# Layer-0 attention: maximum units two to a stretch of scores, one unit's weighing moved, maxima turned in the output bank, inverses in halves

## The reference, cut to what matters

```
q, k, v = x @ w_q, x @ w_k, x @ w_v          # 16 heads of 64
dot = (q / 8) (k / 8)^T                    # scale 1/sqrt(64) on both
att = softmax(where(causal, dot, -inf))
out = att @ v;  return out @ w_u + b_u
x = x + layernorm(attention(layernorm(x)))
```

## Time and profile before

| | before |
|---|---|
| time of three runs, median (lowest to highest) | 2432.9 us (2432.2 to 2436.88) |
| the profiled execution: time, span of its trace | 2433.75 us, 2432.0 us |
| PE busy, share of the span | 2176.9 us, 90% |
| DVE, ACT, POOL busy | 1454.1, 1212.4, 1039.8 us (60%, 50%, 43%) |
| PE busy in 60 to 1080 us, where the pairs run | 954.78 of 1020 us |
| POOL, DVE, ACT busy there | 700.24, 709.24, 514.57 us |

### The profile page before, as it was taken

How to read it: one execution, slowest core, us unless ns; L and a number is a source line. 1 busy time by engine, 2 the same in 40 slices (tenths; PEclk the granted TensorE clock), 3 DMA queues, 4 the chain that set the end, 5 groups by cost and what they waited for, 6 DMA issues and landing times. The chain is left out here.

```text
span 2432.0 us, 41391 instructions
## 1 busy us (share of the span) xinstructions
PE 2176.9 (90%) x15940; PEld 1427.7 (59%) x15940; DVE 1454.1 (60%) x3248; ACT 1212.4 (50%) x1788; POOL 1039.8 (43%) x980
## 2 busy tenths in 40 slices
PE   4999999999999999996899999969999998897787
PEld 2555565555655565554788888734444455555667
DVE  3577757777677757772556665655565455656533
ACT  2455544555365544541333333257787876664533
POOL 0577766777576766774232232423332321100001
PEclk9999999999999999998899999979999999999999
DMA  2000000000000000000300000000000000002001
GB/s 75 1 1 1 1 1 1 1 1 1 2 1 1 1 1 1 1 1 1 73 1 1 1 1 1 1 1 1 1 1 1 1 1 1 2 8 70 1 1 35
DMA packets 36327, 18.26 MB, mean 8 GB/s; under 512 B 16666, under 2 KB 33956, under 8 KB 36132
## 3 DMA queue, kind: packets, MB, share of 16 engines
q1 hardware_dynamic: 36132, 15.61, 2.5%
HBM read 13.50 MB, written 2.10 MB: 6 GB/s over the span
## 5 line engine op out<-in xcount | busy, mean ns | idle before, releaser
L331 POOL TENSOR_TENSOR a_first<-a_first,a_ring 128x512 f32<-128x512 f32 (+3 forms) x352 | 556.4, 1581 | 289.2 <-PE a_o_ps L511 248.4
L1820 ACT ACTIVATE g_probsT<-g_s_ps 128x1024 f32<-128x1024 f32 (+2 forms) x448 | 369.0, 869 | 136.9 <-PE g_s_ps L1689 82.6
L608 ACT ACTIVATE a_ring<-a_st 128x768 f32<-128x768 f32 (+1 forms) x256 | 228.2, 918 | 118.4 <-PE a_st L496 117.1
L511 PE MATMUL a_o_ps<-a_ring,a_v 128*64 128x512 f32 (+3 forms) x1280 | 231.7, 483 | 2.9 <-POOL a_ring L313 2.8
L699 DVE RECIPROCAL a_row_inv<-a_row_inv 128x512 f32<-128x512 f32 x64 | 214.1, 3345 | 20.9 <-ACT a_row_inv L596 20.9
L1090 ACT ACTIVATE m_silu<-m_up,m_b 128x512 f32<-128x512 f32 x160 | 109.8, 689 | 220.4 <-PE m_up L1022 217.6
L1720 PE MATMUL g_o_ps<-g_probsT,g_values 128*32 128x512 f32 (+5 forms) x2688 | 206.7, 419 | 5.5 <-POOL g_probsT L1565 5.1
L684 DVE CUSTOM_DVE_ANT_0 a_masked<-a_mx,mask_wide,a_part_max 128x256 bf16<-128x256 f32 (+3 forms) x256 | 128.4, 548 | 128.3 <-PE a_mx L467 128.3
L467 PE MATMUL a_mx<-a_k_hi,a_q_hi 64*128 64x512 f32 (+3 forms) x768 | 155.1, 419 | 51.6 <-DVE a_largest L684 24.0
L1689 PE MATMUL g_s_ps<-g_qT,g_kT 64*128 64x512 f32 (+3 forms) x896 | 173.5, 434 | 27.5 <-ACT g_probsT L1820 21.4
L1565 POOL TENSOR_SCALAR_AFFINE_SELECT g_probsT<-g_probsT 128x512 f32<-128x512 f32 x128 | 88.2, 692 | 244.9 <-ACT g_probsT L1820 244.8
(11 more groups left out here) (315 smaller groups left out, 4470.4 us busy)
## 6 DMA issues: line engine op xcount, KB each, us to landing
m_w<-in_L_ffn_rw SPq DMA_DIRECT2D x2, 1024.0 KB, 8.3
s_w<-in_L_ffn_w SPq DMA_DIRECT2D x1, 2048.0 KB, 9.6
s_w<-in_L_ffn_w SPq DMA_DIRECT2D x4, 512.0 KB, 10.4
out_x<-x SPq DMA_DIRECT2D x8, 256.0 KB, 2.3
m_w<-in_L_ffn_rw SPq DMA_DIRECT2D x2, 512.0 KB, 5.2
x<-in_L_attn_x SPq DMA_DIRECT2D x1, 512.0 KB, 4.6
a_outT<-in_L_attn_w_q SPq DMA_DIRECT2D x1, 512.0 KB, 5.3
a_outT<-in_L_attn_w_k SPq DMA_DIRECT2D x1, 512.0 KB, 6.0
```

The source lines that it names most:

```text
L331: pool.tensor_tensor(total[:, h, q:q + w], total[:, h, q:q + w], probs_of(n, u)[:, h, off:off + w], ALU.add).then_inc(added, 1)
L511: last = pe.matmul(o_ps[rows_of(h), first_q:first_q + w], v_half[n // 4 % 2][:, j, head:head + A_HD], probs_of(n, u)[:, h, off:off + w], s ...
L608: act.activation(probs_of(n, u)[:, :, 0:w], st_ps[u % 2][:, :, 0:w], ACT.Exp).then_inc(exp_done, 1)
L1820: act.activation(out, src.rearrange("p k (j n) -> p k j n", j=at_once), ACT.Exp, scale=float(HD) ** -0.5).then_inc(exp_done, 1)
```

## The change

- Maximum units stand two to a phase, one ahead of the scores (from phase 2 on) and one behind them; none stands between S0 and S1. M7 moves to the phase 4 before.
- W3 moves from phase 2 to phase 3, ahead of W4; R0 goes with it, between W4 and W5; R1 moves behind W1.
- T0 is written into `a_o_ps`, after ACT has kept chunk 0's output, and last in phase 2. W3, the next to write that bank, waits for `keep_shift`.
- The V's of a pair are both made in `a_p_ps`, in phases 3 and 4; those of the first half batch, made before pair 0, go to four slots in the score banks.
- DVE's inverses come in halves of 256 columns, in phases 1 to 4, one to a phase; at a batch's first pair both halves of a chunk stand together, in phases 1 and 2.
- `scale_output` of chunk 0 moves in POOL's list from u = 3 to u = 6, that of chunk 1 from u = 6 to behind u = 9 (u = 8 at a batch's first pair).
- The variance of a layer norm is three pieces in three phases, and the normalisation on ACT of a batch's input is moved to the pair after, that of its output to phase 4.

PE's order in a plain pair becomes
M8 S0 S1 M9 W8 W9 P T1 | S2 M0 S3 M1 W0 W1 R1 P | M2 S4 S5 M3 W2 P T0 | M4 S6 S7 M5 W3 W4 R0 W5 V | M6 S8 S9 M7 V W6 W7 P.

PE in pair 0, from behind S5, before: the maximum unit M2 (`a_mx<-a_k_hi,a_q_hi`), W2, R0 (L442), W3 (`a_first`), T0, P and M3.

The diff, cut to its core:

```diff
-MAXES_FIRST = {0: (0, 7), 2: (1, 1), 3: (1, 3), 4: (1, 5)}
-MAXES_MIDDLE = {0: (0, 8), 1: (1, 0)}
-MAXES_LAST = {0: (0, 9), 2: (1, 2), 3: (1, 4), 4: (1, 6)}
+MAXES_FIRST = {0: (0, 8), 2: (1, 2), 3: (1, 4), 4: (1, 6)}
+MAXES_MIDDLE = {1: (1, 0)}
+MAXES_LAST = {0: (0, 9), 1: (1, 1), 2: (1, 3), 3: (1, 5), 4: (1, 7)}
-INVERSES = {1: 0, 2: 1}
-FINISHING = {1: {3: (0, 2), 4: (2, 5)}, 2: {4: (5, 7)}}
-NORMALIZING = {2: {3: (0, 4)}, 3: {1: (4, 5)}}
+INVERSES = {1: (0, 0), 2: (0, 1), 3: (1, 0), 4: (1, 1)}
+FINISHING = {1: {3: (0, 2), 4: (2, 4)}, 2: {0: (4, 5), 1: (5, 6), 2: (6, 7)}, 3: {0: (7, 9)}}
+NORMALIZING = {2: {3: (0, 2), 4: (2, 4)}, 3: {1: (4, 5), 2: (5, 6), 3: (6, 7)}}
...
+def inverses_of_phase(n, t):
+
+    if not 0 <= n - 1 < ALL_PAIRS:
+        return []
+    if n % PAIRS == 0:
+        return [(n - 1, c, part) for c in range(2) for part in range(2) if t == 1 + c]
+    return [(n - 1, *INVERSES[t])] if t in INVERSES else []
...
-                        if n and u == 3:
+                        if n and u == 6:
                             scale_output(n - 1, 0)
-                        if n and u == 6:
+                        if n and u == 8 and n % PAIRS == 0:
                             scale_output(n - 1, 1)
...
+                        if n and u == 9 and n % PAIRS:
+                            scale_output(n - 1, 1)
...
-                    if k == 1:
-                        if m > 1:
-                            pe.wait_ge(sums_kept, 2 * (m - 1))
-                        for half, blk in values_of_phase(m - 1, 1) if m else ():
-                            pe.wait_ge(v_kept, NB * half + blk + 1)
+                    if k == 2 and m > 1:
+                        pe.wait_ge(sums_kept, 2 * (m - 1))
+                    if k == 3:
+                        pe.wait_ge(qk_hi_done, 4 * m + 3)
                     if k == 5:
                         pe.wait_ge(qk_hi_done, 4 * m + 4)
-                    if k == 3:
-                        pe.wait_ge(qk_hi_done, 4 * m + 3)
-                        pe.wait_ge(shift_kept, 2 * m + 1)
-                        if m:
-                            pe.wait_ge(sums_kept, 2 * m - 1)
+                    if k == 6 and m:
+                        pe.wait_ge(sums_kept, 2 * m - 1)
...
                 def turn_maxima(m, c):
                     pe.wait_ge(max_ready, 2 * m + c + 1)
+                    if c == 0 and m:
+                        pe.wait_ge(o_kept, 2 * m - 1)
+                    out = mx_ps[:, 0, :] if c else o_ps[:]
...
+                    if u == FIRST_OF_CHUNK[1] and n + 1 < ALL_PAIRS:
+                        pe.wait_ge(shift_kept, 2 * n + 3)
...
                     if t == 2 and 0 <= n < ALL_PAIRS:
                         weigh(n, 2)
+                    if t == 3 and 0 <= n < ALL_PAIRS:
+                        weigh(n, 3)
+                        weigh(n, 4)
                         add_rows(n, 0)
-                        weigh(n, 3)
...
                         if running and t == 2:
                             keep_output(n, 0)
+                        if running and t == 3:
                             keep_sums(n, 0)
...
-                def invert_sums(n, c):
+                def invert_sums(n, c, part):
+                    cols = slice(part * HALF // 2, (part + 1) * HALF // 2)
                     dve.wait_ge(sums_kept, 2 * n + c + 1)
-                    dve.reciprocal(row_inv[c][:], row_inv[c][:]).then_inc(inv_ready, 1)
+                    dve.reciprocal(row_inv[c][:, cols], row_inv[c][:, cols]).then_inc(inv_ready, 1)
```

More of the change, by code:

```diff
@@ L56, in statistics, with spreads @@
             chain.did(dve.bn_stats(t.stats[:, blk, :], x_of(blk)))
-    def variance():
+    def spreads():
         chain.settle()
@@ L75, in normalize, with variance @@
                                         ALU.subtract, ALU.mult))
+    def variance():
+        spreads()
+        means()
+        total()
     quarters = [range(blk, blk + 2) for blk in range(0, NB, 2)]
-    return [*(lambda q=q: statistics(q) for q in quarters), variance,
+    return [*(lambda q=q: statistics(q) for q in quarters), *((spreads, means, total) if apart else (variance,)),
             *(lambda q=q: normalize(q) for q in (range(0, 4), range(4, NB))), chain.settle]
@@ L150, in values_of_phase @@
     if n < 0:
-        return [(0, blk) for blk in {1: (0, 1), 2: (2, 3), 3: (4, 5), 4: (6, 7)}.get(t, ())]
-    if half >= HALVES or t not in (1, 3):
+        return [(0, blk) for blk in {0: (0, 1), 1: (2, 3), 2: (4, 5), 3: (6, 7)}.get(t, ())]
+    if half >= HALVES or t not in (3, 4):
         return []
-    return [(half, n % 4 * 2 + t // 3)]
-def values_in_maxima(n, t):
-    return n >= 0 and t == 1
+    return [(half, n % 4 * 2 + t - 3)]
 def outputs_of_phase(n, t):
@@ L554, in _ @@
                             turn_input(b, c)
+                        if n >= 0 and t == 4:
+                            for half, blk in values_of_phase(n, t):
+                                project_values(half, blk)
                         for b, part in outputs_of_phase(n, t):
@@ L565, in _ @@
                             turn_maxima(n, 1)
+                        if t == 2 and m < ALL_PAIRS:
+                            turn_maxima(m, 0)
+                        if n < 0 or t == 3:
+                            for half, blk in values_of_phase(n, t):
+                                project_values(half, blk)
             @block.scalar
@@ L624, in _ @@
                             exponentials(n, 2 * t)
+                        if n > 0 and t == 1:
+                            keep_sums(n - 1, 1)
+                        if running:
                             exponentials(n, 2 * t + 1)
@@ L627, in _ @@
                             keep_input(b, c)
+                        if n >= 0 and t == 4:
+                            for half, blk in values_of_phase(n, t):
+                                keep_values(half, blk)
                         if n > 0 and t == 0:
                             keep_output(n - 1, 1)
-                        if n > 0 and t == 1:
-                            keep_sums(n - 1, 1)
                         if running and t == 2:
                             keep_output(n, 0)
+                        if running and t == 3:
                             keep_sums(n, 0)
[L635 to L638, removed]
                         for of, k in projections_of_phase(n, PROJECTED_IN, t):
@@ L642, in _ @@
                             keep_shift(n, 1)
-                        if n % PAIRS == 2 and n > PAIRS and t in BLOCKS_FINISHED:
-                            for start in BLOCKS_FINISHED[t]:
+                        if m < ALL_PAIRS and t == 2:
+                            keep_shift(m, 0)
+                        if n < 0 or t == 3:
+                            for half, blk in values_of_phase(n, t):
+                                keep_values(half, blk)
+                        if n % PAIRS == 2 and n > PAIRS and t == 4:
+                            for start in (0, 4):
                                 normalize_blocks(y, y, y_normed, 2 * (n // PAIRS), start)
-                        if n % PAIRS == 3 and n // PAIRS + 1 < BATCH and t in BLOCKS_NORMALIZED:
+                        if n % PAIRS == 4 and n // PAIRS + 1 < BATCH and t == 0:
                             b = n // PAIRS + 1
@@ L649, in _ @@
                                 act.wait_ge(residual_done, 2 * (b - 1))
-                            for start in BLOCKS_NORMALIZED[t]:
+                            for start in (0, 4):
                                 normalize_blocks(x_norm, g.x[:, b * NB:(b + 1) * NB, :], x_normed, 2 * b - 1, start)
@@ L782, in _ @@
                             add_bias(b, part)
-                        if t in INVERSES and 0 <= n - 1 < ALL_PAIRS:
-                            invert_sums(n - 1, INVERSES[t])
+                        for of, c, part in inverses_of_phase(n, t):
+                            invert_sums(of, c, part)
                         for piece in pieces_of_phase(n, t):
```

57 lines of the change are left out of this document (29 added, 28 removed).

## The result

The changed kernel takes 2535.68 us (median; 2532.76 to 2537.66) against 2434.89 us; the ratio, here and below one of mean times, is 1.0404, with a 95% interval of 1.037 to 1.0439. It is slower by 4%, 2.3 us from the forecast of 2538. The profiled execution has a span of 2535.9 us, against 2432.0.

A forecast was written before the change was run, and what follows sets the result against it. PE was taken to set the pace, waiting 2.3 us a pair. Pairs +68, clock +39, ahead of pair 0 -8, batch ends +5 and pair 31 +2 gave +106 on 2433.75; forecast 2538 us, range 2480 to 2584.

The forecast's parts named there:

- pairs 1 to 27, longer wait at the full clock: Pairs 1 to 27: 33.4 us each against 31.13, which is +2.2 a pair (+1.6 to +2.7).
- behind pair 31's T1: Pair 31: POOL's list sets PE's pace from a later W3, with one scaling more ahead of the last sums: +2.
- M6: Maximum unit M6 waits through ACT's copy for POOL's late scaling, starting 8.2 after W3, not 4.6: 3.6 us standing.
- What goes: PE's waits at M8, M9, R0, M1 and M3 all go, 2.3 us a pair, leaving 28.8 us of work.
- M1: Maximum unit M1, with only S3 between it and M0, waits for DVE's reads: 0.6 us a pair.
- T0, M2, M5: Small waits in each pair, at M2 and T0 0.1 each, at M5 0.2: together 0.4 us.
- The clock: Idle time at M6 lowers PE's clock; 2.0 us a fall, one in three passing without: +39 over 30 pairs.
- the clock falls in every pair: Rival: a fall of the clock in every pair at the full price, 2.7 us: 2582 us, chance 0.13.
- The batch ends: Three batch ends: 4.04 us waits go, against later inverses, scaling, variance and normalisations: +5 (-12 to +18).
- Ahead of pair 0: Before pair 0: four slots end V's and P's waits for ACT's copy, one maximum pair more exposed: -8 (-5 to -15).
- the clock holds: Rival: the 3.6 us of idle time doesn't lower the clock: 2501 us, chance 0.17.
- the scaling is in time: Rival: `keep_sums` doesn't wait for POOL's scaling, a pair is 1.3 shorter: 2394 us, up to 2420, chance 0.10.

The follow-up runs named there:

- experiment 1: The changed kernel with POOL scaling chunk 0's output ahead of the sums of units 4 and 5 (u == 4): 2422.8 us, ratio 0.9949.
- experiment 2: The changed kernel with chunk 0's scaling between the sums of units 4 and 5 (u == 5): 2453.64 us, ratio 1.0073.
- experiment 7: The kernel before with POOL's order alone changed, chunk 0's scaling at u == 6, chunk 1's at u == 8: 2670.04 us, ratio 1.0963.
- experiment 6: The changed kernel with 24 idle matmuls in each pair between V and the wait at M6: 2489.0 us, ratio 1.0224.
- experiment 8: Experiment 5's kernel with POOL cutting the diagonals of units 7, 8 and 9 one sum sooner each: 2374.83 us, ratio 0.9747.
- experiment 5: Experiment 1's kernel, turned inputs one phase later, chunk 1's output at a batch's first pair scaled at u == 6: 2393.45 us, ratio 0.9823.
- Experiment 4: The kernel before with only the first half batch's values made in four score-bank slots, a phase sooner: 2417.57 us, ratio 0.9928.

## Why the prediction was right, term by term

The mechanism is shown: experiments 1, 2 and 7 move the scaling alone, and PE's wait follows it. What each term of the sum measured, by the starts of ACT's copy of T1's shifts in each pair of the traces before, after and of experiment 6 (1019.8 us from pair 0's to pair 31's before, 1132.9 after, 1087.5 with the wait filled):

The clock's row is the traces after and of experiment 6 compared in pairs 1 to 30; the batch ends' is what is left of those pairs, with the falls of the clock that experiment 6 still has there.

| term | predicted | measured |
|---|---|---|
| pairs 1 to 27, longer wait at the full clock | 27 x 2.2 = 60 | 27 x (32.81 - 31.13) = 45 |
| pairs 28 to 30, the same | 8 | 7 |
| the clock | 39 | 47 |
| ahead of pair 0, and pair 0 | -8 | -11 and -1 |
| batch ends | +5 | +14 |
| behind pair 31's T1 | +2 | +2 |
| sum | +106 | +104, of unrounded terms |

- *M6.* 8.16 us after W3 and 3.6 us of waiting in 27 pairs: as forecast, in each step. In pairs 28 to 30 it was 4.5.
- *What goes.* M8's, M9's and R0's waits are gone, as forecast.
- *M1.* 0.36 marked as idle in experiment 6's pair, that is 0.56 by starts, against 0.6.
- *T0, M2, M5.* This step failed in size: 0.4 us a pair were put down, and experiment 6's plain pair shows no wait at them. PE's own work was put at 28.8; experiment 8's pair of 29.16, with M1's 0.55 as its only wait, leaves 28.6. So a pair at the full clock was 32.8 and not 33.4. Had it been as forecast, the time would have been some 15 us above.
- *The clock.* The step was "one in three passes without a fall" and 2.0 us for a fall. The runs showed a fall in each of the 30 pairs, at 1.58 us. Both factors were off, in opposite directions; that the product, 1.3, was near is luck. The rival that the clock falls in every pair had the count right and the price (2.7) wrong.
- *The batch ends.* The 4.04 us waits went, as forecast. But the turned inputs, moved to phases 1 and 2, were not costed: 2.83 us of waiting in three pairs and a fall of the clock behind some. In experiment 5 the inputs stand a phase later and the wait is gone. The other part, the later scaling ahead of the output product, was named, and in the changed kernel it is covered by M6's wait.
- *Ahead of pair 0.* -11 against -8. Experiment 4 shows that the new values' slots alone bring 15 to 17, most of it clock. Why this trace of the changed kernel keeps only 11 of them was not tested by a run, but the other traces say something: six experiments have its list up to that copy unchanged, and from PE's first matmul to the copy they take 36.4 to 39.7 us, the changed kernel's trace 40.9, the kernel before 51.6. In these six, matmuls of 512 columns first take 0.4 to 0.5 us between 31.8 and 37.3 us, in the changed kernel's at 49.7. So a part of the difference varies from one execution to the next, with the clock.
- *The other rivals.* That the clock holds is out (granted clock 0.95 over a plain pair). That the scaling is in time was to give 2394 to 2420; experiment 1 put it in time and gave 2422.8. Its plain pair, 29.90, is as short as the rival's 31.13 - 1.3, with a wait at W7 and not at W9; pairs 28 to 30 and the batch ends are what it lacks.
- *The addition.* 2433.75 + 106 - 0.85 is 2539, and 2538 was given; that changes nothing.

The mechanism and the 3.6 us at M6 were right. That the total came within 3 us is luck: 15 us too much in the pairs stand against 8 too little for the clock and 9 too little at the batch ends.

## What to carry to other kernels

When an instruction moves in one engine's list, follow its result through every engine up to the one that sets the pace, also for results that only free a buffer: here the copy of new row sums waited for the *use of the old ones*, and a scaling that nobody needed soon held PE for 3.6 us a pair from the last place where one would look. Price it from the rows in which the same instructions stand in the new order already. An idle time on TensorE can cost more than itself, and filling it with idle matmuls is a cheap test of how much; and a wait removed uncovers the next one, so ask what it had hidden before counting the whole gain.

## What the runs showed of the hardware

Adding matmuls made the kernel faster: 24 idle ones in each of 31 pairs took 47 us off, since the clock stayed at 2.4 GHz. The idle times of 3.6 to 4.5 us at M6, in an otherwise busy stream, had a stretch of the lower clock in or just behind them 30 times in 30; the three of 2.83 us at the turned inputs in the same trace once; those of 1.1 us in experiment 2 never in a plain pair. And the granted clock of a window may be wrong early in a trace: from 28 to 71 us in the kernel before it reads 1.00 (windows, the granted clock third from the end):

```profile
28.00:71.00 43.00, 30.14 (x83) 16.21 (x83) 15.61 (x44) 10.20 (x16) 0.82 (x2) 1.00 0.00 1
```

Yet the matmuls there took as long as at the lower clock elsewhere (0.79 for the first of a projection's, against 0.50 at the full one). There, the matmuls' own durations are the safer reading.
